# Prologue order of a recursive interaction kernel: c1 chunks ahead of D, weight passes re-ordered, first loads on one queue, D's last stores issued by ScalarE

## The chip, the cores and the metric

One core of a Trainium2 chip. The metric is the device time of one execution in microseconds (us), as the median of several runs.

## The reference

Batch 512, 40 features, depth 16, three layers of 100 units. Cut to what matters:

```python
for Wk, bk in zip([W0, W1, W2], [b0, b1, b2]):
    z = jnp.einsum('bid,bjd->bdij', base, curr)
    curr = jnp.einsum('bdij,ijh->bhd', z, Wk) + bk[None, :, None]
    logit.append(curr)
pooled = jnp.sum(jnp.concatenate(logit, axis=1), axis=-1)
out = pooled @ lin_w + lin_b
```

The kernel uses that only a weighted sum of the third layer is wanted. It forms the products x_a * x_b of all pairs of features (with a feature of ones added, 41 in all) once, and multiplies them by two sets of weights: W0, which gives the first layer (c1), and a set Q folded from W1, W2 and the linear weights, which gives a second factor. The output is the sum over units and depth of c1 times that second factor, plus a constant.

## The kernel before

**Tiles.** The columns are depth times batch; one unit u of the loop is 1024 columns (two depths), 8 units in all. The 861 pairs are laid out as 7 chunks of 126 partitions, so there are 56 chunks, m = 7u + c. For each chunk VectorE multiplies the two x tiles (`form`, L263), ScalarE rounds the product to fp32r (`round_high`, L367), VectorE subtracts to get the rest (`split`, L270), and TensorE multiplies by W0 into c1_ps (`c1_chunk`) and by Q into q_ps (`q_chunk`). Each of these two is three passes of two matmuls (`chunk_products`, L499): high weights by high product, low weights by high product, high weights by low product. Per unit, ScalarE copies c1 out and VectorE multiplies and adds (`product`). The order on each engine is written out by hand; the engines meet by semaphores.

**The first unit.** In the first 30 us everything is built at once. The first tile of x comes in halves: xa by SyncE (L185), xb by ScalarE (`load_first_xb`, L391). For chunks 1 to 5 the x_b rows aren't loaded but selected by TensorE from chunk 0's (`select_xb`, L543) into PSUM, where `form` reads them; chunk 6 is loaded. The weights W0 come as pairs (i, j) and (j, i) in four pieces (`load_w0`, cut at chunks 0, 1, 3, 5): GpSimd adds them (`sum_w0`, L459), ScalarE rounds (`cast_w0`, L386), GpSimd subtracts (`low_w0`, L465).

**Q's weights.** TensorE makes V from W2 and the linear weights (`v_piece`, L558 and L564), ScalarE copies it, TensorE turns it (`turn_v`, L573), ScalarE copies again (L412). Then D = V times W1 in five groups (`d_group`, L588 and L591) in the order 4, 0, 1, 2, 3, using two PSUM banks in turn, so that a group waits for the copy of the one before last. The copies (`copy_d`) are ScalarE's, but for group 2, VectorE's (L301). D goes to DRAM in ten stores (`store_d`, L172): eight issued by SyncE, two by GpSimd behind `dgroup_copied` 3, that is behind the copy of group 1. After all ten have landed and GpSimd has cleared part of the tile (L480, behind its last `low_w0`), twelve gathers bring D back as pairs (`gather_d`, L166): seven issued by SyncE, five by ScalarE, which has them ahead of chunk 7's rounding. VectorE makes the Q weights of chunks 0 to 3 in two pieces (`first_weights`: sum L308, high L311, low L313), GpSimd those of chunks 4 to 6. Behind the gathers SyncE loads the second unit's x. ScalarE raises `q_psum_free`, for which the first Q chunk waits, ahead of chunk 7.

TensorE's own order is: warm-up matmuls, selections 1 and 2, V pieces 0 and 1, c1 chunk 0, V pieces 2 and 3, the constant, selection 3, turning V, selection 4, D groups 4, 0, 1, selection 5, D groups 2, 3, c1 chunks 1 to 6, Q chunks 0 to 6, and from chunk 7 on c1 and Q in turn.

## Time and profile before

| | us |
|---|---|
| median of 3 runs (180.68 to 181.23) | 181.17 |
| profiled execution | 181.1 |
| its span | 179.3 |
| TensorE matmul busy (97%) | 173.2 |
| VectorE busy (86%) | 153.5 |
| ScalarE busy (41%) | 73.1 |
| GpSimd busy (7%) | 13.2 |

The span is the time from the first to the last instruction of the program in one profiled execution; that execution took 1.8 us more than its span. Matmuls are pipelined and their ends are modelled, so what counts for TensorE is where it starts to wait. An entry in square brackets behind an instruction is the idle time of its engine in front of it and what ended it. [...]

### The profile page before, as it was taken

How to read it: one execution, taken by the hardware profiler on the slowest of the kernel's cores; microseconds unless marked ns; L12 is line 12 of the kernel's file. 1: busy time of each engine (PE TensorE's matmuls, PEld its weight loads, DVE VectorE, ACT ScalarE, POOL GpSimd, SP SyncE). 2: the span in 40 equal slices, each digit the busy share in tenths (PEclk: the TensorE clock that was granted, in tenths of full speed). 3: DMA queues.
4: the chain of work that ended last, by engine and by line, in shares of the span. 5: the costliest groups of instructions: out<-in, count | busy, mean ns of one | idle time of the engine just before them, and what ended most of it. 6: DMA issues, size and time to landing. Idle time of an engine off the chain costs nothing.

```text
span 179.3 us, 2565 instructions
## 1 busy us (share of the span) xinstructions
PE 173.2 (97%) x800; PEld 118.2 (66%) x800; DVE 153.5 (86%) x141; ACT 73.1 (41%) x80; POOL 13.2 (7%) x22
## 2 busy tenths in 40 slices
PE   6899987999999999999999999999999999999995
PEld 1273655777777777777777777777777777777762
DVE  0799976399999999999999999999999999994012
ACT  2556710064642464336432644264425542530020
POOL 3253904000000000000000000000000000000000
PEclk9999999999999999999999999999999999999999
DMA  5999744999878677857785779577947740000000
GB/s 165 396 411 399 263 103 121 419 413 412 280 237 301 158 230 230 325 133 236 229 302 163 228 228 310 162 224 236 327 134 227 229 149 0 0 0 4 0 0 0
DMA packets 12636, 37.59 MB, mean 210 GB/s; under 512 B 2548, under 2 KB 3668, under 8 KB 12628
## 3 DMA queue, kind: packets, MB, share of 16 engines
q1 hardware_dynamic: 11408, 36.39, 61.2%
q10 hardware_dynamic: 1156, 0.85, 1.8%
q0 software_dynamic: 64, 0.25, 0.4%
q8 instruction: 5, 0.08, 0.2%
q14 instruction: 3, 0.02, 0.0%
HBM read 36.40 MB, written 1.07 MB: 209 GB/s over the span
## 4 chain that ended last, share of the span: by engine, by line
PE 85%; DMA 6%; DVE 4%; SPq 2%; issue 1%; ACT 0%; DVEq 0%
PE q_ps L499 42%; PE c_ps L499 39%; DMA x_a<-xa 3%; DVE xb_z L263 2%; DMA pair_sb<-d_dram 2%; SPq L172 1%; DMA d_dram<-w_d 1%; PE q_ps L564 1%; PE q_ps L508 1%; PE c_ps L543 1%; SPq L166 1%; PE c_ps L638 1%; PE q_ps L543 1%; PE c_ps L642 0%; DVE acc L356 0%
## 5 line engine op out<-in xcount | busy, mean ns | idle before, releaser
L367 ACT ACTIVATE z_high<-xb_z 126x1024 fp32r<-126x1024 f32 x56 | 59.3, 1061 | 80.2 <-DVE xb_z L263 78.9
L270 DVE TENSOR_TENSOR z_low<-xb_z,z_high 126x1024 fp32r<-126x1024 f32 x56 | 69.2, 1241 | 0.5 <-ACT z_high L367 0.5
L263 DVE TENSOR_TENSOR xb_z<-x_a,xb_z 126x1024 f32<-126x1024 f32 x50 | 61.3, 1226 | 3.3 <-DMA xb_z<-xw 3.2
L499 PE MATMUL c_ps<-z_high,wc_high 126*101 126x512 f32 x112 | 35.3, 396 | 0.6 <-DVE z_low L270 0.6
L499 PE MATMUL c_ps<-z_low,wc_high 126*101 126x512 f32 x112 | 35.0, 394 | 0.0
L499 PE MATMUL c_ps<-z_high,wc_low 126*101 126x512 f32 x112 | 35.0, 393 | 0.0
L499 PE MATMUL q_ps<-z_high,wq_high 126*101 126x512 f32 x108 | 34.0, 396 | 0.9 <-DVE wq_low L313 0.9
L499 PE MATMUL q_ps<-z_high,wq_low 126*101 126x512 f32 x108 | 33.8, 394 | 0.0
L499 PE MATMUL q_ps<-z_low,wq_high 126*101 126x512 f32 x108 | 33.7, 393 | 0.0
L499 PEld LDWEIGHTS c_ps<-z_high,wc_high 126*101 126x101 f32 x112 | 18.3, 165 | 9.0 <-ACT z_high L367 1.1
L499 PEld LDWEIGHTS c_ps<-z_high,wc_low 126*101 126x101 f32 x112 | 18.5, 165 | 7.5
L499 PEld LDWEIGHTS c_ps<-z_low,wc_high 126*101 126x101 f32 x112 | 18.5, 165 | 7.4
L499 PEld LDWEIGHTS q_ps<-z_high,wq_high 126*101 126x101 f32 x108 | 17.8, 165 | 8.5 <-DVE wq_low L313 1.4
L499 PEld LDWEIGHTS q_ps<-z_high,wq_low 126*101 126x101 f32 x108 | 17.9, 165 | 7.3
L499 PEld LDWEIGHTS q_ps<-z_low,wq_high 126*101 126x101 f32 x108 | 17.8, 165 | 7.2
L374 ACT ACTIVATE w_post<-c_ps 101x1024 f32<-101x1024 f32 x8 | 8.1, 1010 | 13.5 <-PE c_ps L499 13.5
L284 DVE TENSOR_TENSOR w_post<-q_ps,w_post 101x256 f32<-101x256 f32 (+1 forms) x3 | 1.4, 508 | 10.5 <-PE q_ps L508 10.5
L280 DVE TENSOR_TENSOR acc<-acc,w_post 101x1024 f32<-101x1024 f32 x7 | 8.6, 1225 | 0.2
L278 DVE TENSOR_TENSOR w_post<-q_ps,w_post 101x1024 f32<-101x1024 f32 x7 | 8.5, 1217 | 0.0
L552 PE MATMUL q_ps<-warm_sb 128*128 128x512 bf16 x14 | 5.7, 587 | 1.6 <-POOL warm_sb L452 1.6
L291 DVE TENSOR_TENSOR xb_z<-x_a,xb_z 126x512 f32<-126x512 f32 x2 | 1.4, 692 | 5.1 <-DMA x_a<-xa 5.1
L552 PEld LDWEIGHTS q_ps<-warm_sb 128*128 128x128 bf16 x14 | 1.5, 104 | 5.4 <-issue 5.4
(59 smaller groups left out, 62.9 us busy)
## 6 DMA issues: line engine op xcount, KB each, us to landing
xb_z<-xw SPq DMA_DIRECT2D x50, 512.0 KB, 4.4
x_a<-xa SPq DMA_DIRECT2D x7, 512.0 KB, 4.8
w_post<-w1x SPq DMA_DIRECT2D x4, 512.0 KB, 8.7
w_d<-w2h SPq DMA_DIRECT2D x4, 404.0 KB, 6.4
pair_sb<-w_pairs SPq DMA_DIRECT2D x3, 202.0 KB, 9.9
xb_z<-xw ACTq DMA_DIRECT2D x2, 256.0 KB, 4.3
x_a<-xa SPq DMA_DIRECT2D x2, 256.0 KB, 4.5
d_dram<-w_d SPq DMA_DIRECT2D x2, 189.4 KB, 3.4
```

Of the source, the lines that this page charges most:

```text
L166: eng.dma_start(q_sides[P * t:P * (t + 1), side, c0 * J:c1 * J].rearrange("p (c j) -> p c j", j=J), src).then_inc(dpair_loaded[piece], 16)
L172: eng.dma_start(d_dram[r0:r1, column * J:(column + n) * J], w2_d[DR * upper + r0:DR * upper + r1, first * J:(first + n) * J]).then_inc(sto ...
L263: nc.vector.tensor_tensor(xb_z[0:K, c, :], x_a[0:K, u % 2, :], x_b, ALU.mult).then_inc(z_done, 1)
L270: nc.vector.tensor_tensor(z_low[0:K, m % SLOTS, :], xb_z[0:K, c, :], z_high[0:K, m % SLOTS, :].bitcast(fp32), ALU.subtract).then_inc(low_d ...
L278: nc.vector.tensor_tensor(prod, q_ps[u % 2][0:J, :], c1_sb[u % 2], ALU.mult).then_inc(q_psum_free, 1)
L280: nc.vector.tensor_tensor(acc[:, :], acc[:, :], prod, ALU.add).then_inc(acc_done, 1)
L367: nc.scalar.activation(z_high[0:K, m % SLOTS, :], xb_z[0:K, m % C, :], ACT.Copy).then_inc(high_done, 1)
L374: nc.scalar.activation(c1_sb[u % 2], c1_ps[u % 2][0:J, :], ACT.Copy).then_inc(c1_copied, 1)
L499: last = nc.tensor.matmul(ps[0:J, h * B:(h + 1) * B], w[0:K, c * J:(c + 1) * J], z[0:K, slot, h * B:(h + 1) * B], start=(c == 0 and k == 0 ...
L508: last = nc.tensor.matmul(q_ps[1][0:J, cols], w[0:K, c * J:(c + 1) * J], z[0:K, slot, cols], start=False, stop=(c == C - 1 and k == 2))
L543: last = nc.tensor.matmul(sel_ps[m % 2][:, cols], select_r[:, m:m + 128], x_split[0:K, cols], start=True, stop=True)
L552: nc.tensor.matmul(warm_ps, warm_sb[:, 0:128], warm_sb[:, :], start=True, stop=True)
```

## The change

- The first halves of xb are issued by SyncE between those of xa, not by ScalarE.
- The second piece of W0 is loaded ahead of W2.
- TensorE: c1 chunk 0 goes ahead of V's pieces and c1 chunk 1 ahead of D's groups; selections 3, 4 and 5 change places (3 ahead of V piece 3, 4 ahead of turning V, 5 behind D's groups); the constant goes behind the first copy of D by VectorE, ahead of c1 chunk 4.
- A chunk's passes are now high by high, high by low product, low weights by high product. The wait for the low products stands ahead of the second pass, the one for low weights ahead of the third; ahead of the first only the high ones are waited for.
- VectorE: forms and splits of the first unit in another order, with the copy of group 2 behind split 3.
- ScalarE: the cast of the second piece of W0 ahead of rounding 2; rounding 3 ahead of the copies of D; rounding 4 between the copies of groups 1 and 3; the constant's copy behind the gathers' issue, with a wait.
- The two stores of group 3 are issued by ScalarE behind its copy of that group, ahead of two casts of W0 and roundings 5 and 6, no longer by SyncE.

```diff
--- before.py
+++ after.py
@@ -184,6 +184,10 @@
                 cols = slice(h * B, (h + 1) * B)
                 sp.dma_start(x_a[:, 0, cols], xa[:, cols]).then_inc(loaded, 16)
 
+            def load_first_xb(h, loaded):
+                cols = slice(h * B, (h + 1) * B)
+                sp.dma_start(xb_z[:, 0, cols], xw[0:128, cols]).then_inc(loaded, 16)
+
             def load_xb(u, c):
                 sp.dma_start(xb_z[:, c, :], xw[c:c + 128, bass.ds(u * N, N)]).then_inc(xb_loaded[c], 16)
 
@@ -200,12 +204,14 @@
                 sp.dma_start(w1_post[:, cols], w1x[:, cols]).then_inc(w1_loaded[i], 16)
 
             load_first_xa(0, xa_first)
+            load_first_xb(0, xb_first)
             load_first_xa(1, xa_loaded[0])
+            load_first_xb(1, xb_loaded[0])
             sp.dma_start(small_sb[:, :], small).then_inc(small_loaded, 16)
             load_w0(0)
+            load_w0(1)
             for i in range(VP):
                 load_w2(i)
-            load_w0(1)
             for i in W1_ORDER:
                 load_w1(i)
             load_w0(2)
@@ -221,9 +227,6 @@
             store_d(sp, 0, LEFT + 2 * GI, 2 * GI, GI, (0, DB))
             store_d(sp, 1, LEFT + UPPER_AT[2], 2 * GI, GI, (DR - DB, DR))
             store_d(sp, 1, 0, 3 * GI - (LEFT - 2 * GI), LEFT - 2 * GI, (0, 32))
-            sp.wait_ge(dgroup_copied, 4)
-            store_d(sp, 0, LEFT + 3 * GI, 3 * GI, GI, (4, 4 + DB))
-            store_d(sp, 1, LEFT + UPPER_AT[3], 3 * GI, GI, (10, 10 + DB))
             sp.wait_ge(equals_cleared, 1)
             sp.wait_ge(d_stored, 16 * DS_SP)
             sp.wait_ge(d_stored_pool, 16 * DS_POOL)
@@ -330,15 +333,16 @@
             form(0, 1)
             form(0, 2)
             split(0, 1)
+            form(0, 3)
             split(0, 2)
-            form(0, 3)
             form(0, 4)
+            split(0, 3)
+            copy_d(2)
+            split(0, 4)
             form(0, 5)
-            copy_d(2)
-            split(0, 3)
             form(0, 6)
-            for m in range(4, C):
-                split(0, m)
+            split(0, 5)
+            split(0, 6)
             first_weights(0)
             first_weights(1)
             products(0, C, 2 * C)
@@ -386,17 +390,11 @@
                 nc.scalar.activation(chunks(wc_high, WC_CUTS[i], WC_CUTS[i + 1]),
                                      w0_sides[0:K, WC_CUTS[i]:WC_CUTS[i + 1], 0, :], ACT.Copy).then_inc(wc_highs, 1)
 
-            def load_first_xb(h, loaded):
-                cols = slice(h * B, (h + 1) * B)
-                act.dma_start(xb_z[:, 0, cols], xw[0:128, cols]).then_inc(loaded, 16)
-
             def round_xa(h, loaded):
                 cols = slice(h * B, (h + 1) * B)
                 act.wait_ge(loaded, 16)
                 nc.scalar.activation(x_split[0:K, cols], x_a[0:K, 0, cols], ACT.Copy).then_inc(xa_high, 1)
 
-            load_first_xb(0, xb_first)
-            load_first_xb(1, xb_loaded[0])
             round_xa(0, xa_first)
             round_xa(1, xa_loaded[0])
             act.wait_ge(small_loaded, 16)
@@ -404,23 +402,26 @@
             round_high(0, 0)
             cast_w0(0)
             round_high(0, 1)
+            cast_w0(1)
             round_high(0, 2)
             act.wait_ge(v_multiplied, 1)
             nc.scalar.activation(v_rows[:, :], v_ps, ACT.Copy).then_inc(v_rows_copied, 1)
-            act.wait_ge(const_done, 1)
             act.wait_ge(v_turned, 1)
             nc.scalar.activation(v_sb[:, :], vt_ps, ACT.Copy).then_inc(v_copied, 1)
-            nc.scalar.activation(const_sb[:, :], const_ps, ACT.Identity, bias=linb,
-                                 scale=float(D)).then_inc(const_copied, 1)
-            cast_w0(1)
+            round_high(0, 3)
             copy_d(4)
             copy_d(0)
             copy_d(1)
-            round_high(0, 3)
+            round_high(0, 4)
             copy_d(3)
+            act.wait_ge(dgroup_copied, 4)
+            store_d(act, 0, LEFT + 3 * GI, 3 * GI, GI, (4, 4 + DB))
+            store_d(act, 1, LEFT + UPPER_AT[3], 3 * GI, GI, (10, 10 + DB))
             cast_w0(2)
             cast_w0(3)
-            for m in range(4, BODY):
+            round_high(0, 5)
+            round_high(0, 6)
+            for m in range(C, BODY):
                 if m == GATHER_AT:
                     act.wait_ge(equals_cleared, 1)
                     act.wait_ge(d_stored, 16 * DS_SP)
@@ -429,6 +430,10 @@
                         if (side, t, piece) not in GATHER_SP:
                             gather_d(act, side, t, piece)
                 if m == C:
+                    act.wait_ge(const_done, 1)
+                    nc.scalar.activation(const_sb[:, :], const_ps, ACT.Identity, bias=linb,
+                                         scale=float(D)).then_inc(const_copied, 1)
+                    act.wait_ge(const_copied, 1)
                     act.wait_ge(z_done, C)
                     act.sem_inc(q_psum_free, 2)
                     act.sem_inc(c1_psum_free, 2)
@@ -491,20 +496,19 @@
 
         @block.tensor
         def _(pe):
-            def chunk_products(ps, high, low, m):
+            def chunk_pass(ps, w, z, m, first, last):
 
                 c, slot = m % C, m % SLOTS
-                for k, (w, z) in enumerate(((high, z_high), (low, z_high), (high, z_low))):
-                    for h in range(2):
-                        last = nc.tensor.matmul(ps[0:J, h * B:(h + 1) * B], w[0:K, c * J:(c + 1) * J],
-                                                z[0:K, slot, h * B:(h + 1) * B],
-                                                start=(c == 0 and k == 0), stop=(c == C - 1 and k == 2))
-                return last
+                for h in range(2):
+                    end = nc.tensor.matmul(ps[0:J, h * B:(h + 1) * B], w[0:K, c * J:(c + 1) * J],
+                                           z[0:K, slot, h * B:(h + 1) * B],
+                                           start=(c == 0 and first), stop=(c == C - 1 and last))
+                return end
 
             def last_q(m, cols):
 
                 c, slot = m % C, m % SLOTS
-                for k, (w, z) in enumerate(((wq_high, z_high), (wq_low, z_high), (wq_high, z_low))):
+                for k, (w, z) in enumerate(((wq_high, z_high), (wq_high, z_low), (wq_low, z_high))):
                     last = nc.tensor.matmul(q_ps[1][0:J, cols], w[0:K, c * J:(c + 1) * J], z[0:K, slot, cols],
                                             start=False, stop=(c == C - 1 and k == 2))
                 return last
@@ -512,24 +516,34 @@
             def c1_chunk(it, m):
                 u, c = divmod(m, C)
                 if m in WC_CUTS[:-1]:
-                    pe.wait_ge(wc_ready, WC_CUTS.index(m) + 1)
+                    pe.wait_ge(wc_highs, WC_CUTS.index(m) + 1)
                 pe.wait_ge(high_done, it * BODY + (m + 1))
-                pe.wait_ge(low_done, it * BODY + (m + 1))
                 if c == 0 and u >= 1:
                     pe.wait_ge(c1_psum_free, it * 2 + (u + 1))
-                last = chunk_products(c1_ps[u % 2], wc_high, wc_low, m)
+                chunk_pass(c1_ps[u % 2], wc_high, z_high, m, True, False)
+                pe.wait_ge(low_done, it * BODY + (m + 1))
+                chunk_pass(c1_ps[u % 2], wc_high, z_low, m, False, False)
+                if m in WC_CUTS[:-1]:
+                    pe.wait_ge(wc_ready, WC_CUTS.index(m) + 1)
+                last = chunk_pass(c1_ps[u % 2], wc_low, z_high, m, False, True)
                 if c == C - 1:
                     last.then_inc(c1_done, 1)
 
             def q_chunk(it, m):
                 u, c = divmod(m, C)
+                if m in PREP_CUTS[:2]:
+                    pe.wait_ge(wq_highs, PREP_CUTS.index(m) + 1)
+                if m == PREP_CUTS[2]:
+                    pe.wait_ge(last_highs, 1)
+                if c == 0:
+                    pe.wait_ge(q_psum_free, it * 2 + (u + 1))
+                chunk_pass(q_ps[u % 2], wq_high, z_high, m, True, False)
+                chunk_pass(q_ps[u % 2], wq_high, z_low, m, False, False)
                 if m in PREP_CUTS[:2]:
                     pe.wait_ge(wq_ready, PREP_CUTS.index(m) + 1)
                 if m == PREP_CUTS[2]:
                     pe.wait_ge(last_ready, 1)
-                if c == 0:
-                    pe.wait_ge(q_psum_free, it * 2 + (u + 1))
-                chunk_products(q_ps[u % 2], wq_high, wq_low, m).then_inc(z_slots_free, 1)
+                chunk_pass(q_ps[u % 2], wq_low, z_high, m, False, True).then_inc(z_slots_free, 1)
 
             def select_xb(m):
 
@@ -578,8 +592,6 @@
                 d_bank = d_ps[place % 2]
                 if place == 0:
                     pe.wait_ge(v_copied, 1)
-                if place == 1:
-                    pe.wait_ge(const_copied, 1)
                 pe.wait_ge(w1_loaded[g], 16)
                 if place > 1:
                     pe.wait_ge(dgroup_copied, place - 1)
@@ -597,22 +609,25 @@
                 warm()
             select_xb(1)
             select_xb(2)
+            c1_chunk(0, 0)
             v_piece(0)
             v_piece(1)
-            c1_chunk(0, 0)
             v_piece(2)
+            select_xb(3)
             v_piece(3)
-            constant()
-            select_xb(3)
+            select_xb(4)
             turn_v()
-            select_xb(4)
+            c1_chunk(0, 1)
             d_group(4)
             d_group(0)
             d_group(1)
-            select_xb(5)
             d_group(2)
             d_group(3)
-            for m in range(1, C):
+            select_xb(5)
+            for m in range(2, C):
+                if m == PREP_CUTS[2]:
+                    pe.wait_ge(dgroup_copied_dve, 1)
+                    constant()
                 c1_chunk(0, m)
             for m in range(C):
                 q_chunk(0, m)
```

## Rows read from the trace of the kernel before

**Rows 1.** The page: its head, clock by slice, and one group by line
```profile
span 179.3 us, 2565 instructions
...
PEclk9999999999999999999999999999999999999999
...
L367 ACT ACTIVATE z_high<-xb_z 126x1024 fp32r<-126x1024 f32 x56 | 59.3, 1061 | 80.2 <-DVE xb_z L263 78.9
```

**Rows 2.** Chain of waits to 45 us: start, duration (us), what
```profile
1.22 5.24 DMA x_a<-xa
...
20.25 0.71 SPq L172
...
21.47 2.09 DMA d_dram<-w_d
...
24.83 2.85 DMA pair_sb<-d_dram
...
28.41 0.38 DVE wq_low L313
...
28.83 10.03 PE q_ps L499 x42
38.86 1.39 PE c_ps L499 x6
```

**Rows 3.** Timeline, TensorE: start, duration, engine, line, work [idle before it <- releaser]
```profile
13.97 0.30 PE L588 MATMUL q_ps<-w_post,v_sb 101*64 101x101 f32 x1
...
17.25 0.13 PEld L588 LDWEIGHTS q_ps<-w_post,v_sb 101*64 101x64 f32 x1 [0.41 <-DMA w_post<-w1x]
...
17.54 0.59 PE L588 MATMUL q_ps<-w_post,v_sb 101*64 101x505 f32 x1
...
28.83 0.71 PE L499 MATMUL q_ps<-z_high,wq_high 126*101 126x512 f32 x2 [0.94 <-DVE wq_low L313]
```

**Rows 4.** Timeline, VectorE, splits (L270) and forms (L263)
```profile
14.46 1.21 DVE L263 TENSOR_TENSOR xb_z<-x_a,c_ps 126x1024 f32<-126x1024 f32 x1
...
18.55 1.74 DVE L270 TENSOR_TENSOR z_low<-xb_z,z_high 126x1024 fp32r<-126x1024 f32 x1
20.21 1.60 DVE L263 TENSOR_TENSOR xb_z<-x_a,xb_z 126x1024 f32<-126x1024 f32 x1
...
36.70 1.22 DVE L270 TENSOR_TENSOR z_low<-xb_z,z_high 126x1024 fp32r<-126x1024 f32 x1
```

**Rows 5.** Timeline, ScalarE and (ACTq) its DMA issues
```profile
0.75 0.90 ACTq L391 DMA_DIRECT2D xb_z<-xw  x2
...
16.10 0.59 ACT L381 ACTIVATE w_d<-q_ps 128x505 f32<-128x505 f32 x1 [0.25 <-PE q_ps L591]
...
18.60 0.59 ACT L381 ACTIVATE w_d<-q_ps 128x505 f32<-128x505 f32 x1 [0.96 <-PE q_ps L591]
19.09 0.62 ACT L386 ACTIVATE wc_high<-pair_sb 126x202 fp32r<-126x202 f32 x2
...
23.62 2.32 ACTq L166 DMA_DIRECT2D pair_sb<-d_dram  x5
```

**Rows 6.** Timeline, GpSimd (L172 stores, L465 low parts, L480 clearing)
```profile
14.31 0.67 POOL L465 TENSOR_TENSOR wc_low<-pair_sb,wc_high 126x202 fp32r<-126x202 f32 x1 [0.85 <-ACT wc_high L386]
17.00 1.14 POOL L172 DMA_DIRECT2D d_dram<-w_d  x2 [2.02 <-ACT w_d L381]
...
17.64 0.50 POOL L172 DMA_DIRECT2D d_dram<-w_d  x1
...
19.54 1.20 POOL L465 TENSOR_TENSOR wc_low<-pair_sb,wc_high 126x202 fp32r<-126x202 f32 x1 [0.34 <-ACT wc_high L386]
...
20.69 1.57 POOL L465 TENSOR_TENSOR wc_low<-pair_sb,wc_high 126x202 fp32r<-126x202 f32 x1
...
22.32 0.17 POOL L480 MEMSET pair_sb<- 42x101 f32 x1
```

**Rows 7.** DMA issues by line: size, us from issue to landing
```profile
d_dram<-w_d POOLq DMA_DIRECT2D x1, 126.2 KB, 4.6
```

## The prediction, made from the kernel before alone

> **What bounds the kernel now.** I read the head of the page first, then the chain of waits, then each engine's timeline up to 30 us. The span is 179.3 us at a granted clock of 9 tenths or more throughout [rows 1]. The chain of waits shows two parts. From 28.83 us on TensorE never waits: 10.03 us of Q matmuls, then chunks of 1.39 us [rows 2], without a gap until the last product. Nothing after 28.83 us changes in amount, so the whole change is worth what it does to one number: **the start of the first Q matmul**. In front of it, read backwards: the weights' split on VectorE (low part 28.41 to 28.79), the gather of D from DRAM (ScalarE's share issued from 23.62 [rows 5], the piece that lands last 2.85 us after 24.83 [rows 2]), the last store of D (issued 21.47, landed 2.09 us later, at 23.56 [rows 2]), D's groups, and the loads of x. TensorE itself is idle for 0.94 us just in front of it [rows 3], with c1 chunks 0 to 6 done. So work moved around on TensorE matters only where D's chain waits for it.
>
> **The change, part by part.**
>
> *Pass order.* A Q chunk now begins with the two passes on the high weights and needs the low weights only 0.93 us later. The high weights are there when the low ones begin, at 28.41; the first matmul started at 28.83 [rows 2]. That removes 28.83 - 28.41 = **0.42 us**, and it is the surest term: no engine is in the way, the low part is done 0.38 us later and is wanted after 0.93. The number of matmuls is the same. A c1 chunk gets one wait ahead of it and one inside it instead of two ahead; the c1 chunks of before carry two waits and Q chunks none, and both take 1.39 us [rows 2], so I take the waits in the loop at nothing. Their bounds: 0, and some 0.04 us (a loop of 14 chunk pairs shows no more than that at its turn) for each of four rounds.
>
> *x's halves on one queue.* SyncE issues xa, xb, xa, xb instead of xa, xa beside ScalarE's xb, xb. One issue is 0.45 us (the two of ScalarE took 0.90 [rows 5]), so small data and the first weights are issued 0.9 us later. The half of xa issued in front of them took 5.24 us to land in a full queue [rows 2], so the issue hides. The last half of xa landed 5.24 us after 1.22, at 6.46; it closes the same four halves in either order, and VectorE wants all four before the second split. I take 0 us; the bounds are -0.5 (halves are no longer interleaved) and +0.5 us (the fourth is issued 0.9 us later). The Trainium skill ("DMA: Bandwidth & Descriptors", "Issuing engines are not separate DMA queues") says that transfers of all issuing engines run on the same 16 DMA engines and only issue time is saved by using several; by that the term is 0 too, and the rule would count against expecting anything from this edit or from the two stores' new queue except their issue time.
>
> *c1 chunks ahead of D.* Chunk 0 trades places with V's first two pieces, which changes no sum. ScalarE gets a cast of 0.31 us (half of 0.62 [rows 5]) ahead of its copy of V's rows, of which some 0.16 is seen, since the copy had waited for rounding 2. D's first group stood behind ScalarE's copy of V and began at 13.97 [rows 3]; TensorE is done turning V some 0.4 us before that. Now c1 chunk 1, 1.39 us, stands **in front of D's first group**: it begins then at 13.97 - 0.56 + 0.16 + 1.39 = 14.96 (0.56: the copy of V and its handing over, under which the chunk runs): D's groups 4, 0 and 1 are 1.0 us later and the copy of group 1 moves from 16.10 to 17.1, its end from 16.69 to 17.7 [rows 5]. But the last two groups were held up by something else: group 3's weights waited for the load of its data until 17.25 and it began at 17.54 [rows 3]. Now it waits for the copy that ends at 17.7 and begins at 17.8. So group 3's copy moves only from 18.60 [rows 5] to 18.85, and group 2's copy on VectorE stays near 18.0. The selection for chunk 5, which went ahead of group 2, comes behind group 3 and ends at 19.4; form 5 is 3 us later than it was.
>
> *The stores.* Before, SyncE issued seven stores behind the copy of group 1, the last at 21.47. Now its last is the third of group 2, issued at 20.25 as before [rows 2]; the two of group 3 leave ScalarE from 19.5 to 20.4 (0.45 each). Before, SyncE's last store took 2.09 us to land [rows 2]; with that and up to 0.4 more, all eight are down at 22.5 to 22.9 instead of 23.56: **0.7 to 1.0 us earlier**. What is late next? Two things, both behind the copy of group 1, which is 1.0 us later. First, GpSimd's stores (issued 17.00 to 18.14 [rows 6]) move to 18.03 and on; the second, begun at 17.64 [rows 6], took 4.6 us to land [rows 7], 17.64 + 1.03 + 4.6 = **23.3**. Second, GpSimd's low parts of W0 and the clearing of the diagonal, which ended at 22.49 [rows 6], and which gathers wait for as well.
>
> *GpSimd against VectorE.* The low part of two chunks took 0.67 us at 14.31 with VectorE from 14.46 on a form that reads PSUM, and 1.20 and 1.57 us at 19.54 and 20.69 [rows 6] while VectorE ran a split and a form that read two SBUF operands; those took 1.74 and 1.60 us instead of 1.22, the PSUM form 1.21 [rows 4]. I read this as turns: each engine's instruction runs alone, some 0.5 us of GpSimd then some 1.15 us of VectorE. Put forward: ScalarE is free of its stores at 20.4, casts chunks 3 and 4 by 20.85 and 5 and 6 by 21.35. The sums are done by 20.95. Form 5 reads PSUM (20.0 to 21.2), so the first low part runs at once, 20.95 to 21.45; form 6 goes next, to 22.6; the second low part to 23.1; the clearing, 0.17 us [rows 6], to **23.3**. Queued behind the two stores on ScalarE are these casts, and roundings 5 and 6; rounding 6 ends at 23.7 (22.65 + 1.06 [rows 1]), so ScalarE's five gathers are issued 0.1 us later than at 23.62. They took 2.32 us for five [rows 5], and SyncE's chain ended last before, so this is covered for 0.6 us or so.
>
> *Sum.* Gather at 23.35 instead of 23.62, less 0.02 for a late start on ScalarE: 0.25 us. Pass order: 0.42. Together **0.67 us**. TensorE is ready for it: its chunk 6 ends at 26.6. c1 7 needs its low part 0.46 us after its start, which was there at 37.92 before [rows 4]; the low part is wanted at 28.16 + 10.03 + 0.46 = 38.65: no stall. The moved constant costs TensorE 0.2 us inside an idle stretch. The profiled execution took 181.1 us for its span of 179.3; 181.1 - 0.67 = 180.43, and the median of the runs is 0.07 above the profiled one: **180.5 us**. A measurement can tell about 0.3%, 0.54 us, from no change.
>
> **The rivals.**
>
> *The gate does not move* (180.75). GpSimd's second store took 4.6 us to land [rows 7] where SyncE's last took 2.09 [rows 2]. If the second lands at 23.6, only the 0.42 of the pass order is left, 181.17 - 0.42. For it: VectorE is more often on two SBUF operands after 18.7 us than it was at 17 to 18. Against: the delay of 1.03 is all that the trace supports.
>
> *GpSimd misses its turn* (slower, 182.0). If the first low part is not under way when form 6 starts at 21.2, it waits for form 6 (22.4), runs to 22.9, then VectorE's split 5 takes its turn to 24.05, the second low part runs to 24.55, and the clearing ends at 24.8. The gather starts 1.2 us later than before: -0.42 + 1.22 = 0.8 us slower. It decides at one point: the cast for chunks 3 and 4 must end before form 6 starts, 20.85 against 21.2, a margin of 0.35 us. Each store issue on ScalarE that takes 0.6 instead of 0.45 eats 0.15 of it, and so does a late first load, which now runs 1 : 1 through V and D. Against it: VectorE may itself wait for a rounding just then and leave the turn to GpSimd. The Trainium skill ("SBUF — State Buffer", "SBUF: two separate sides") states that VectorE with two SBUF operands and GpSimd take a shared port pair by an exclusive lock, the loser waiting for the whole instruction; by that rule a miss costs what is worked out here, and if they shared it by halves instead it would cost 0.3 us or so. The stretched rows agree with the lock.
>
> *The stores were everything* (179.9). If GpSimd's stores need not shift with their issue, and its low part runs while VectorE waits, the gather starts at 22.9 less 0.1: 0.42 + 0.8 = 1.2 us off.
>
> *The clock falls.* TensorE would stand idle from 26.6 to 28.2 us, longer than the gaps of before [rows 3], under which the clock stayed [rows 1]. If it fell, matmuls at 1.2 GHz would add perhaps 1 to 2 us. Nothing in the rows speaks for it.
>
> **How the numbers follow.** Forecast 0.42; the gate does not move 0.25; missed turn 0.17; stores were everything 0.10; late first loads or the clock 0.06. The forecast's own range, 180.2 to 180.7, lies for the larger part beyond 0.54 us; the first rival doesn't reach it. Faster: 0.10 + 0.32 of the 0.42 = 0.42. Same: 0.25 + 0.10 = 0.35. Slower: 0.17 + 0.06 = 0.23. The range takes in the missed turn and all but the end of the fast rival: 179.8 to 182.0.
>
> **What would show it.** In the trace after: the first Q matmul on the high weights starts within 0.05 us of the end of the high cast, whatever else happens. The copy of D's group 1 ends at about 17.7 and group 3's at 19.4. SyncE has six stores, ScalarE two from 19.5. GpSimd's clearing ends at 23.3 and its second low part follows form 6; a clearing at 24.8 is the missed turn. SyncE's first gather at 23.35 us confirms the gate, at 23.6 the first rival. TensorE's chunks keep 1.39 us. The prediction is wrong if the first select matmuls do not start near 8.0 us, or if any gap opens after the first Q matmul.

## The result and the profile after

The changed kernel takes **181.86 us** (median of 10 runs, 181.27 to 183.87) beside 180.64 us for the kernel before, re-measured in the same rounds; the ratio is 1.0087, with a 95% interval of 1.0065 to 1.0109. It is 1.2 us slower. The ratio is higher than the medians make it (1.0068), since it also counts by their length three runs in which TensorE's mean granted clock was 0.990 or 0.991 and which lasted 183.22 to 183.87 us; without them the medians differ by 1.15 us and the means by 1.0. The forecast was 180.5 with a range of 179.8 to 182.0: the time lies inside the range, but on the other side of no change, and the chance given to that was 0.23. The profiled execution took 181.72 us for a span of 179.9.

The chain of waits of the kernel after, to 45 us (start, duration, what):

```profile
17.72 0.60 ACT w_d L385
...
18.61 1.15 POOL d_dram L172 x2
...
19.77 1.89 POOL pair_sb L464 x2
...
21.68 0.38 ACT wc_high L390
...
22.13 2.88 POOL wc_low L470 x2
...
25.06 0.18 POOL pair_sb L485
...
25.26 0.36 SPq L166
...
26.47 2.48 DMA pair_sb<-d_dram
...
29.38 0.28 DVE wq_high L314
...
29.70 9.91 PE q_ps L503 x42
```

The first Q matmul starts at 29.70 instead of 28.83 [rows 2]. Read backwards: it follows the high cast by 0.05 us, as forecast. In front of that stand the gather, issued at 25.26 instead of 23.62, GpSimd's clearing (25.06), its two low parts (22.13 to 25.01), ScalarE's cast (21.68), GpSimd's two sums (19.77 to 21.66), its stores (18.61), and the copy of D's group 1 (17.72). Before, the last store of D stood where the clearing stands now. In this execution it is the chain of the rival of the missed turn, which gave 182.0 us and a clearing ended at 24.8; it ended at 25.23. Three more traces with the same order (e14, e9, e15) show another chain; they stand with e4 and e6 below.

The same stretch in the timelines of VectorE, GpSimd and ScalarE of the kernel after:

```profile
19.32 1.45 DVE L273 TENSOR_TENSOR z_low<-xb_z,z_high 126x1024 fp32r<-126x1024 f32 x1
...
21.82 1.21 DVE L266 TENSOR_TENSOR xb_z<-x_a,xb_z 126x1024 f32<-126x1024 f32 x1
...
19.77 1.88 POOL L464 TENSOR_TENSOR pair_sb<-pair_sb 126x202 f32<-126x202 f32 x2
22.13 2.87 POOL L470 TENSOR_TENSOR wc_low<-pair_sb,wc_high 126x202 fp32r<-126x202 f32 x2 [0.47 <-ACT wc_high L390]
...
23.43 1.56 POOL L470 TENSOR_TENSOR wc_low<-pair_sb,wc_high 126x202 fp32r<-126x202 f32 x1
...
19.56 0.59 ACT L385 ACTIVATE w_d<-q_ps 128x505 f32<-128x505 f32 x1 [0.31 <-PE q_ps L603]
20.18 1.45 ACTq L172 DMA_DIRECT2D d_dram<-w_d  x2
21.68 0.63 ACT L390 ACTIVATE wc_high<-pair_sb 126x202 fp32r<-126x202 f32 x2 [1.53 <-POOL pair_sb L464]
```

The cast began at 21.68, right when ScalarE had both stores out (20.18 + 1.45), and the first low part at 22.13. The chain and the bracket put the cast down to the sums, but the first cast wants only the first sum, and that was done at 21.16. Form 6, with two SBUF operands, had begun at 21.82. So the low part took 1.34 us where 0.5 to 0.6 is its own work, and the second, behind a split, 1.56 (the two together 2.87). The sums have the same mark: the first waited for split 4, which ran from 19.32; both took 1.88 us, where the timeline of before has 1.04 for the two.

The front of the profile differs too. Busy time, clock and DMA of two stretches of 1 us (after the stretch: its length, then PE, PEld, DVE, ACT, POOL, granted clock, DMA share, GB/s), first the kernel before, then after:

```profile
5.00:6.00 1.00, 1.00 (x4) 0.29 (x3) 0.93 (x2) 0.17 (x1) 0.00 (x0) 1.00 1.01 376
6.00:7.00 1.00, 1.00 (x5) 0.23 (x3) 0.52 (x1) 0.52 (x1) 0.00 (x0) 1.00 1.05 395
```

```profile
5.00:6.00 1.00, 1.00 (x4) 0.28 (x3) 0.59 (x1) 0.25 (x1) 0.00 (x0) 1.00 0.96 295
6.00:7.00 1.00, 0.97 (x3) 0.20 (x3) 0.44 (x1) 0.38 (x1) 0.00 (x0) 1.00 0.96 309
```

The DMA engines are about as busy (0.96 where it was 1.01 and 1.05) and move 22% less: 376 and 395 GB/s became 295 and 309. This isn't chance of one execution: from 5 to 7 us the eight traces with one queue have 285 to 332 GB/s and the nine with two 383 to 403, and from 7 to 9 us 339 to 373 against 398 to 419; by 9 to 12 us the two groups meet (404 to 412 and 406 to 419).

### The profile page after: what moved, and what is told of

Its sections match the earlier page's. It is cut to its first block, busy times and chain, and to the rows that moved or that the text cites. A ratio compares the mean times of both kernels' runs of the same rounds, so it can differ in the third digit from the quotient of the medians.

```text
span 179.9 us, 2514 instructions
## 1 busy us (share of the span) xinstructions
PE 173.3 (96%) x800; PEld 117.9 (66%) x800; DVE 152.6 (85%) x141; ACT 73.2 (41%) x80; POOL 13.8 (8%) x22
## 3 DMA queue, kind: packets, MB, share of 16 engines
HBM read 36.40 MB, written 1.07 MB: 208 GB/s over the span
## 4 chain that ended last, share of the span: by engine, by line
PE 87%; DMA 4%; POOL 3%; DVE 2%; SPq 1%; issue 1%; ACT 1%; DVEq 0%
PE q_ps L503 42%; PE c_ps L503 40%; DMA xb_z<-xw 2%; POOL wc_low L470 2%; DMA pair_sb<-d_dram 1%; POOL pair_sb L464 1%; PE q_ps L578 1%; PE q_ps L512 1%; PE c_ps L557 1%; POOL d_dram L172 1%; PE q_ps L557 1%; SPq L166 1%; PE q_ps L603 1%; PE c_ps L653 1%; PE q_ps L600 1%
## 5 line engine op out<-in xcount | busy, mean ns | idle before, releaser
L470 POOL TENSOR_TENSOR wc_low<-pair_sb,wc_high 126x202 fp32r<-126x202 f32 (+1 forms) x4 | 5.5, 1379 | 2.8 <-ACT wc_high L390 2.8
```

The source lines that it names most:

```text
L470: nc.gpsimd.tensor_tensor(chunks(wc_low, c0, c1), w0_sides[0:K, c0:c1, 0, :], chunks(wc_high, c0, c1).bitcast(fp32), ALU.subtract).then_in ...
```

## The experiments

Each ran beside the kernel before on the same chip. "Low clock" counts runs with a mean granted clock below 0.995. The ratio comes from the single runs, not from the two medians; low-clock runs are part of it in after, e4, e6, e8, e13 and e14, so compare medians there too. One run of e8 took 346.5 us and one of e7 970.2 us, for no cause that the record shows; the medians hardly feel them.

| kernel | median us | before beside it | ratio, 95% interval | low clock |
|---|---|---|---|---|
| after | 181.86 | 180.64 | 1.0087 [1.0065, 1.0109] | 3 of 10 |
| e1 before + pass order | 179.92 | 180.71 | 0.9958 [0.9939, 0.9977] | 0 of 12 |
| e2 before + one queue | 181.52 | 180.71 | 1.0031 [1.0003, 1.0059] | 3 of 12 |
| e3 after, two queues | 181.39 | 180.71 | 1.0034 [1.0011, 1.0058] | 1 of 12 |
| e5 after, c1 chunk 1 behind D | 181.21 | 180.71 | 1.0032 [1.0011, 1.0052] | 0 of 12 |
| e4 after, stores on SyncE | 181.76 | 180.45 | 1.0070 [1.0047, 1.0092] | 2 of 12 |
| e6 after, cleared early | 182.09 | 180.45 | 1.0069 [1.0045, 1.0094] | 2 of 8 |
| e8 e1 + stores ahead of casts | 180.40 | 180.45 | 0.9993 [0.9966, 1.0020] | 1 of 12 |
| e7 e1 + stores behind casts | 180.03 | 180.45 | 0.9958 [0.9939, 0.9978] | 0 of 12 |
| e9 after, 16 warm-ups | 181.62 | 180.66 | 1.0069 [1.0041, 1.0097] | 0 of 7 |
| e10 e3 and e5 together | 180.66 | 180.66 | 1.0000 [0.9981, 1.0019] | 0 of 12 |
| e11 e10, stores behind casts | 180.49 | 180.66 | 0.9986 [0.9968, 1.0004] | 0 of 12 |
| e12 e1, 15 warm-ups | 180.04 | 180.66 | 0.9966 [0.9949, 0.9984] | 0 of 12 |
| e13 before, 10 warm-ups | 182.21 | 180.53 | 1.0105 [1.0064, 1.0145] | 4 of 6 |
| e14 after once more | 182.08 | 180.53 | 1.0107 [1.0066, 1.0148] | 2 of 7 |
| e15 after, 16 warm-ups again | 181.98 | 180.53 | 1.0070 [1.0047, 1.0093] | 0 of 8 |

The theory after the result: the first Q matmul is late because GpSimd's work behind group 1's copy is late and then loses a turn to VectorE. Rivals: ScalarE's stores hold the casts; one queue for x makes everything late; the pass order itself costs; and, as e14 will show, the landing of the last store is late by itself.

### e1: the pass order alone

```diff
-                for k, (w, z) in enumerate(((high, z_high), (low, z_high), (high, z_low))):
+                chunk_pass(c1_ps[u % 2], wc_high, z_high, m, True, False)
+                pe.wait_ge(low_done, it * BODY + (m + 1))
+                chunk_pass(c1_ps[u % 2], wc_high, z_low, m, False, False)
...
+                last = chunk_pass(c1_ps[u % 2], wc_low, z_high, m, False, True)
```

> The kernel before with the pass order and its waits alone (high weights by high and by low product first, low weights last; waits split). By my working, the first Q matmul starts behind the high cast and not behind the low part: 0.42 us earlier than in the kernel before. The trace of the changed kernel shows besides that the turns of the loop cost nothing any more (c1 and Q chunks 1.44 us at a turn of before, six turns, 0.05 each): 0.27 us more. Expected: -0.4 to -0.7 us against before, first Q matmul within 0.05 us of the end of the high cast. Rival: passes only look cheaper because TensorE meets a later wait, and the time doesn't move.

Measured: 179.92 us, 0.8 us below the kernel before beside it. It is the fastest kernel of the case, before and after included. The chain of waits at one turn of the loop and at the same place of the next turn, first the kernel before, then e1 (with its first seven Q chunks):

```profile
55.50 1.41 PE c_ps L499 x6
56.91 1.44 PE q_ps L499 x6
58.34 1.39 PE c_ps L499 x6
...
76.39 1.44 PE q_ps L499 x6
```

```profile
28.75 9.91 PE q_ps L498 x42
...
55.24 1.40 PE c_ps L498 x6
56.64 1.39 PE q_ps L498 x6
58.03 1.40 PE c_ps L498 x6
...
76.11 1.39 PE q_ps L498 x6
```

Before, the chain has six such rows of 1.44 us, one at each turn, where the others are 1.37 to 1.41; e1 has none. From the first Q matmul to the end of the span before took 150.5 us (179.3 - 28.83), e1 150.2 (179.0 - 28.75), the changed kernel 150.2 (179.9 - 29.70). But the rows of 1.44 aren't where the time went: a whole round of the loop takes 19.48 us before (76.39 - 56.91) and 19.47 in e1 (76.11 - 56.64), since other chunks of e1 take 1.40 where those of before take 1.38. Up to TensorE's last matmul it is 148.46 or 148.47 us in the three traces with the old pass order and 148.20 to 148.22 in the fourteen with the new one: 0.26 us less, 0.12 of it in the first seven Q chunks (10.03 and 9.91 to 9.93) and 0.14 spread over the rest. The saving is firm; which part of the edit, the order or the place of the waits, makes it was not tried. In the profiled execution of e1 the stores landed 0.6 us later than in that of before (24.17), which hides the 0.42 us at the first Q matmul there; the median has it.

### e2: one queue alone, and e3: the changed kernel with two

```diff
-            load_first_xb(0, xb_first)
-            load_first_xb(1, xb_loaded[0])
...
             load_first_xa(0, xa_first)
+            load_first_xb(0, xb_first)
             load_first_xa(1, xa_loaded[0])
+            load_first_xb(1, xb_loaded[0])
```

The two lines taken out are ScalarE's, those put in SyncE's. e3 is the reverse of this on the changed kernel.

> The kernel before with the four halves of x on SyncE's queue alone. In the changed kernel the 14 loads of the first 20 us land 0.6 to 1.2 us later than before, and the trace moved 295 to 309 GB/s between 5 and 7 us where the kernel before moved 376 to 395. Theory A (one queue is the cause): here too the loads behind x land 0.6 us later or more, D's group 3 and the last store shift by as much, and the time is 0.5 to 0.7 us longer. Theory B (the bandwidth was that of another execution or chip, not of the queue): loads land as in the kernel before, the time is the same within 0.2 us.

> The changed kernel with xb's halves issued by ScalarE again, all else as changed. If one queue costs the 0.6 us, the loads land as before and the copy of D's group 1 ends 0.4 to 0.6 us earlier, near 17.8 us. If the missed turn of GpSimd is a matter of that shift, the clearing ends at 23.3 to 23.6 instead of 25.2 us and the time falls by 1.5 us or so; if the missed turn comes from c1 chunk 1 ahead of D and from what stands on GpSimd behind group 1's copy, only 0.4 to 0.6 us come back.

Measured: e2 takes 181.52 us, 0.8 more than the kernel before (without the low-clock runs 181.42 against 180.62, the same 0.8). e3 takes 181.39, 0.4 less than the changed kernel without low-clock runs (181.37 against 181.79). Both traces for 5 to 7 us, e2 first:

```profile
5.00:6.00 1.00, 1.00 (x5) 0.28 (x3) 0.93 (x2) 0.00 (x0) 0.00 (x0) 1.00 1.03 337
6.00:7.00 1.00, 0.97 (x3) 0.20 (x3) 0.00 (x0) 0.63 (x1) 0.00 (x0) 1.00 0.92 291
```

```profile
5.00:6.00 1.00, 1.00 (x4) 0.30 (x3) 0.99 (x2) 0.37 (x1) 0.00 (x0) 1.00 1.04 391
6.00:7.00 1.00, 1.00 (x5) 0.23 (x3) 0.94 (x3) 0.85 (x3) 0.00 (x0) 1.00 1.09 404
```

e2 has the low rate on the kernel before, e3 the full one on the changed kernel. Theory A holds: it is the queue. In e2 the last piece of W1 landed at 18.05 us instead of 17.20 and the last store of D at 24.43 instead of 23.56. What the queue costs is less firm: 0.8 us by e2's medians, 0.6 by its ratio with an interval from 0.1 to 1.1, 0.4 by e3, which ran beside other runs than the changed kernel did, and 0.55 by e10 against e5. e3 also answers the second question. Group 1's copy began at 17.24 instead of 17.72, and the clearing still ended at 24.75, a turn late. The missed turn does not come from the queue.

### e5: c1 chunk 1 behind D, and e10: with two queues

```diff
-            c1_chunk(0, 1)
             d_group(4)
...
             d_group(3)
             select_xb(5)
+            c1_chunk(0, 1)
```

> The changed kernel with c1 chunk 1 moved behind D's groups and selection 5. If c1 chunk 1 ahead of D is what makes GpSimd late (it cost 1.0 us up to group 1's copy), that copy ends at 17.2 to 17.4 instead of 18.3 us, GpSimd's stores, sums and low parts follow, the clearing ends near 23.5, and the time falls by 1.2 to 1.7 us against the changed kernel, below the kernel before. If ScalarE's two stores hold the casts up instead, the casts stay at 21.6 us and the time comes down by 0.3 us at most.

> The changed kernel with xb's halves on ScalarE again and c1 chunk 1 behind D's groups: both causes on D's path undone, the stores and the orders left. Sum of the single steps: two queues gave 0.4 us, c1 chunk 1 behind D 0.6: 180.8 us. The copy of group 1 should end at 17.0 to 17.3 us. What would be left against 179.9 (the pass order alone) is then the stores ahead of the casts, 0.5 to 0.6 us, and W0's second piece ahead of W2. If it is 181.2 or more, something else in the orders costs.

Measured: e5 181.21 us, 0.6 below the changed kernel; e10 180.66, 0.7 below e3 on full clock (181.37). In e5 group 1's copy ended at 17.84 us (17.2 to 17.4 expected), the clearing at 23.88 (near 23.5 expected), and the casts began at 21.73, held by ScalarE's stores as the rival said. But the gather started at 24.99: the last of those stores had landed at 24.92. The 0.6 us gained are half or less of what the first theory expected (1.2 to 1.7) and twice what the rival allowed (0.3 at most); the rest went to this next gate. In e10 the gate is the same, with the clearing ended just before it (24.02); the chain of waits:

```profile
19.34 4.75 DMA d_dram<-w_d
...
24.16 0.36 SPq L166
```

The DMA on the gate was issued by ScalarE at 19.34 and landed 4.75 us later. So a store that is issued early is not down early. Eight other stores were under way when it was issued; when the last store of the kernel before was issued at 21.47 and landed 2.09 us later, four were.

### e4: the stores back on SyncE, and e6: no wait for GpSimd's low parts

e4 moves the two stores and their wait from behind `copy_d(3)` on ScalarE back to the end of SyncE's stores. e6 gives the gathered pairs a tile of their own (and puts the output into the old one, which isn't shown):

```diff
+        gathered = sb("gathered", [128, 2 * C * J])
-        q_sides = pair_sb.ap().rearrange("p (s n) -> p s n", s=2)
+        q_sides = gathered.ap().rearrange("p (s n) -> p s n", s=2)
...
+            nc.gpsimd.memset(q_sides[0:P, 1, 0:J], 0.0).then_inc(equals_cleared, 1)
...
-            pool.wait_ge(wc_ready, len(WC_CUTS) - 1)
-            nc.gpsimd.memset(q_sides[0:P, 1, 0:J], 0.0).then_inc(equals_cleared, 1)
```

> The changed kernel with group 3's two stores issued by SyncE again, behind its others. In the changed kernel ScalarE's second store was in issue until 21.63 us and the cast of the third W0 piece began at 21.68, though its sum had been ready at 21.16. Theory C (the stores on ScalarE hold the casts): the casts start at 21.2, GpSimd's low parts a turn earlier, the clearing ends 0.5 us or more earlier, and SyncE's own last store lands at 25 us or later, so that the stores become the gate; the time within 0.3 us of the changed kernel. Theory D (what is late is all on GpSimd, behind group 1's copy): the clearing stays at 25.2 us; the time doesn't fall.

> The changed kernel with the gathered pairs in a tile of their own, cleared at the start by GpSimd, so that the gather waits for the stores alone and for ScalarE to be free, and no longer for GpSimd's low parts. In the changed kernel the last store landed at 24.58 us and the clearing ended at 25.23. If the low parts' missed turn is the gate, the gather starts at 24.6 instead of 25.26 and the time is 0.6 us shorter than the changed kernel's, but still as long as before's or a little longer, since the stores too land 1.0 us later than before's 23.56. If the stores were the true gate, no change.

Measured: e4 181.76 us, no change from the changed kernel. Its chain of waits and GpSimd's timeline:

```profile
22.55 2.36 DMA d_dram<-w_d
...
21.70 0.58 POOL L470 TENSOR_TENSOR wc_low<-pair_sb,wc_high 126x202 fp32r<-126x202 f32 x1
...
23.86 0.18 POOL L485 MEMSET pair_sb<- 42x101 f32 x1
```

The casts began at 21.25, the first low part at 21.70 and took 0.58 us: it caught its turn, and the clearing ended at 24.04, 1.2 us earlier than in the changed kernel. That is what theory C forecast. It also bears out the exclusive lock of the Trainium skill ("SBUF — State Buffer", "SBUF: two separate sides"): the same instruction took 0.58 us where it came before VectorE's and 1.34 where it came behind. But SyncE's own last store was issued at 22.55 and landed at 24.91, and the gather started at 24.98. Either gate is late by itself; taking one away leaves the other 0.3 us behind it. e6 took 182.09 us, 181.94 without its low-clock runs: no gain, as its rival (the stores are the true gate) said. Its profiled execution is one with a low clock and can't be compared step by step; there the gather waited for a store. That the low parts' turn alone is worth 0.6 us is **not shown**.

Three further traces speak against it. e14 is the changed kernel unaltered; e9 and e15 differ from it by two warm-up matmuls. The chain of waits of e14, and GpSimd's timeline:

```profile
20.00 1.33 SPq L172
21.37 3.23 DMA d_dram<-w_d
...
24.67 0.36 SPq L166
...
21.82 0.58 POOL L470 TENSOR_TENSOR wc_low<-pair_sb,wc_high 126x202 fp32r<-126x202 f32 x1
...
23.98 0.18 POOL L485 MEMSET pair_sb<- 42x101 f32 x1
```

The first low part began at 21.82, ahead of form 6 (22.00), took 0.58 us, and the clearing ended at 24.16, all with the two stores still on ScalarE. So e4's caught turn doesn't need e4's edit. The gather waited until 24.67 for SyncE's third store of group 2, issued at 21.37 and landed 3.23 us later. In e9 and e15 the clearing ended at 23.87 and 24.44, and the gather started at 25.17 and 25.56, behind stores that landed at 25.11 and 25.50. GpSimd missed its turn in one of four traces of this order; in the other three the landing of a store was the gate, and in the first too it was only 0.65 us behind the clearing (24.58). Nor does the time follow the turn: the execution that missed it took 181.72 us, the three that didn't 181.26, 181.62 and 182.15.

### e8 and e7: the stores on ScalarE, on a kernel that is otherwise good

```diff
-            sp.wait_ge(dgroup_copied, 4)
-            store_d(sp, 0, LEFT + 3 * GI, 3 * GI, GI, (4, 4 + DB))
-            store_d(sp, 1, LEFT + UPPER_AT[3], 3 * GI, GI, (10, 10 + DB))
...
             copy_d(3)
+            act.wait_ge(dgroup_copied, 4)
+            store_d(act, 0, LEFT + 3 * GI, 3 * GI, GI, (4, 4 + DB))
+            store_d(act, 1, LEFT + UPPER_AT[3], 3 * GI, GI, (10, 10 + DB))
             cast_w0(2)
             cast_w0(3)
```

(e7 has the three lines behind the casts.)

> The kernel before with the pass order (179.9 us) and, besides, group 3's two stores issued by ScalarE right behind its copy, ahead of the casts, as in the change. By my working of the stores, all are down at 22.5 to 22.9 us; in this kernel c1 chunk 1 isn't ahead of D and GpSimd isn't late. If the casts aren't held, the gather starts near 23 and the time is 0.5 to 0.8 us below the pass order alone (179.2). If ScalarE's issue holds the casts by 1 us and GpSimd then misses its turn, the clearing ends at 23.7 to 24.5 and nothing or less is gained (179.9 to 180.4).

> As the one before, but with the two stores behind ScalarE's two casts and ahead of rounding 4: the casts can't be held, the stores are issued 0.6 us later (from 19.8 us). Expected by the theory of the held casts: clearing at 22.5 as in the kernel before, stores landed near 23.2 to 23.6, time 0.3 to 0.7 us below the pass order alone. By the rival (landing is set by the DMA queues and not by who issues): stores land near 24, the time is that of the pass order alone, 179.9.

Measured: e8 180.40 us, that is the time of before, so the whole 0.4% of the pass order is gone; e7 180.03, with e1's ratio of 0.9958. The chain of e8, and e7's:

```profile
19.93 0.84 ACTq L172
...
20.81 0.39 ACT wc_high L383
...
21.26 2.90 POOL wc_low L465 x2
...
24.21 0.19 POOL pair_sb L480
...
24.42 0.36 SPq L166
```

```profile
18.65 1.52 SPq L172
...
20.22 3.19 DMA d_dram<-w_d
...
23.48 0.36 SPq L166
```

e8 shows the mechanism with nothing else changed: store 0.84 us in issue, the cast behind it at 20.81 instead of 19.18 in e1, two low parts of 2.90 us together, the clearing, the gather at 24.42. e7 has the casts free, and its gate is SyncE's third store of group 2: it could be issued only at 20.22, behind one that took 1.52 us, and landed 3.19 us later. Its traced gather starts at 23.48, but its median is e1's within 0.1 us. (e1's profiled execution, 180.78 us, lay 0.9 above its median, so the traces of the two don't compare.) The expectation by the theory, 0.3 to 0.7 us below the pass order alone, missed. The stores on ScalarE bring nothing there. Ahead of the casts they cost 0.4 us by the medians of e8 and e7, which ran side by side, and 0.35% by the ratios, whose intervals overlap a little.

### e11: the changed kernel with all three mended

> As the one before, with ScalarE's two stores behind its two casts. If the stores ahead of the casts cost what they cost on the kernel before (0.5 us), 180.3 us, and the clearing ends before the last store has landed; if the gate is the stores' landing by now, no gain, 180.8.

Measured: 180.49 us, 0.9986 [0.9968, 1.0004]. The 0.1% gained on e10 (0.2 us by the medians) is within the intervals. The casts were free (from 19.93 us) and the clearing ended at 22.72, but the gather waited until 23.74 for ScalarE's second store, landed at 23.68. Against e7 (0.9958), which has the stores in the same place, the other moves of the change (selections, forms and splits, W0's second piece, the constant) would cost 0.28%, 0.5 us; the two intervals overlap, and which move it would be was not tried.

### e9, e12 to e15: the clock

All change WARM alone, the number of warm-up matmuls (e12 on e1, e13 on the kernel before, the others on the changed one).

> The changed kernel with 16 warm-up matmuls instead of 14. In the trace of the changed kernel TensorE is idle for 1.01 us between the warm-up and the first selection (0.76 before the change), and 3 of its 10 runs have a mean clock of 0.991 and last 183.2 to 183.9 us instead of 181.8. In one trace of an experiment with such a clock the clock stood at half for 3.4 us from 8.6 us on, after 1.74 us of idle time there. Theory: that idle stretch is what lets the clock fall; with two more matmuls it shrinks to 0.3 us, no run of 12 has the lower mean clock, and the median of the others stays at 181.8. Rival: the clock falls for another cause (the idle before the first Q matmul, or the chip): 2 to 4 of 12 runs still show it.

> A version to beat both kernels: the kernel before with the pass order alone and 15 warm-up matmuls instead of 14. Expected 179.9 us as without the added matmul (it runs where TensorE was idle for 0.5 to 0.8 us), and no run with a lower mean clock. If the 15th matmul delays the first selection, 180.0 to 180.3.

> The kernel before with 10 warm-up matmuls instead of 14: TensorE is idle 1.5 us longer ahead of the first selection (2.3 instead of 0.8 us), nothing else changes. Theory (that idle stretch lets the clock fall): far more runs than before's 4 in 95 have a mean clock of 0.991 or less, each some 2 us longer; if most have, the median goes to 182.5. Rival (another cause): one run of 12 at most, median 180.6.

> The changed kernel once more, unaltered, beside the next one on the same chip. Median 181.8, 2 to 4 of 12 runs with a clock of 0.991 and 183 us or more. If none has it, the share depends on the chip.

> The changed kernel with 16 warm-up matmuls again, for more runs. Theory of the idle stretch: no run with a low clock, median of the rest within 0.2 us of the one before. Rival: as many low runs as the one before.

Measured: the count is in the table. The trace of e6 and that of e13 caught the fall. TensorE's timeline at the first selection, and the granted clock of three stretches, for e6 and then e13:

```profile
8.85 1.19 PE L557 MATMUL c_ps<-z_high,select_r 126*128 126x512 f32 x2 [1.74 <-DVE z_high L300]
...
5.20:8.60 3.40, 1.88 (x6) 0.43 (x5) 2.01 (x4) 1.40 (x3) 0.47 (x1) 1.00 0.95 326
8.60:12.00 3.40, 3.15 (x8) 2.35 (x9) 2.98 (x4) 1.16 (x3) 2.08 (x3) 0.51 1.03 407
12.00:16.00 4.00, 4.00 (x77) 2.74 (x75) 2.87 (x3) 2.04 (x4) 1.35 (x1) 0.99 1.03 412
```

```profile
8.02 0.71 PE L543 MATMUL c_ps<-z_high,select_r 126*128 126x512 f32 x2 [1.98 <-DVE z_high L296]
...
8.60:12.00 3.40, 3.40 (x40) 2.46 (x39) 3.40 (x4) 1.20 (x2) 1.26 (x2) 0.61 1.05 412
12.00:16.00 4.00, 4.00 (x49) 2.58 (x49) 3.58 (x3) 1.95 (x6) 1.67 (x2) 0.90 1.02 409
```

TensorE stood idle for 1.74 and 1.98 us ahead of the first selection, and the granted clock went from 1.0 (2.4 GHz) to 0.5 (1.2 GHz): at 8.6 us in e6, still in the idle stretch, and between 9 and 10 us in e13, when TensorE had been at work again for over 1 us. It was back by 12 or shortly after. e2's trace has an idle stretch of 1.84 us at the same place and no fall, so the stretch alone doesn't decide it. In e6 the pair of selections took 1.19 us instead of 0.70. Such runs of the changed kernel last 183.2 to 183.9 us, 1.4 to 2.1 more than its median without them.

Counted over all runs: kernels with one queue and 14 warm-ups 12 of 61 (after, e14, e2, e4, e5, e6); with 16 warm-ups 0 of 15; the kernel before 5 of 109; with 10 warm-ups 4 of 6; the kernels with two queues, the new pass order and 14 warm-ups (e1, e3, e7, e8, e10, e11) 2 of 72. The two extra warm-ups cut the idle stretch from 1.0 to 1.3 us (after and e14) to 0.2 to 0.8 us (e9 and e15). Fewer warm-ups clearly raise the share. More warm-ups point the same way, but at a share of 12 in 61, none in 15 would come up by chance about once in 27 times. So the idle stretch ahead of the first selection goes with the fall of the clock, and in the kernel before making it longer brought the fall on. In e13 the four low-clock runs took 182.0 to 182.6 us, 1.5 to 2.1 more than the kernel before beside it, but its two others 181.4 and 183.9, of which I have no account. With 16 warm-ups the median hardly moves (181.98 in e15 beside 182.08 in e14); the tail is what goes. e12 took 180.04 us, no better than e1, which had no low-clock run either.

## Why the prediction was wrong

**The step that failed in every trace is the landing of D's last store.** The sum had SyncE's and ScalarE's stores down at 22.5 to 22.9 us, GpSimd's at 23.3, and the gather at 23.35. In the four traces of this order the last store landed at 24.58, 24.60, 25.11 and 25.50 (23.56 before) and the gather started between 24.67 and 25.56. (GpSimd's landed at 23.39, as forecast.) Two queues again, c1 chunk 1 behind D as well, and the stores behind the casts as well brought it to 24.20, 24.10 and 23.68 (e3, e10, e11), so as far as single traces can tell three terms fed it: one queue for x, c1 chunk 1 ahead of D, and the price of a store.

**Pass order: right in mechanism, too small.** 0.42 us by the high cast; e1 shows 0.8 us (ratio 0.9958). The step "I take the waits in the loop at nothing" allowed only for a cost, and for four rounds where the chain shows six turns; measured is a gain of 0.26 us behind the first Q matmul, 0.12 of it in the first seven Q chunks. With 0.42 that makes 0.7. Why those chunks are shorter is open.

**One queue: the first step that failed.** I took 0 with bounds of 0.5 us. e2 shows 0.8 us on the kernel before (0.6 by the ratio), e3 0.4 on the changed one. The working counted bytes ("the same four halves in either order") and asked whether issues hide. They do: nothing waited for an issue. What changed is the rate up to about 9 us; why is open. The rule of the Trainium skill ("DMA: Bandwidth & Descriptors", "Issuing engines are not separate DMA queues") that several issuing engines only save issue time would make this term 0 as well; here the measurement decides against it, with 285 to 332 GB/s on one queue and 383 to 403 on two.

**c1 chunk 1 ahead of D: right in size, wrong in what followed.** It was forecast to put group 1's copy 1.0 us later, ending at 17.7; it ended at 18.31, the rest from the queue (17.83 in e3, with two). Then I said that it matters only up to group 3's load. e3 against e10 shows 0.7 us (e5 against the changed kernel 0.6): what stands behind group 1's copy, GpSimd's stores, sums and low parts, was taken for uncritical, and in e5 the clearing came 1.35 us earlier (23.88).

**The stores: wrong.** "0.45 each" was taken from loads issued at the very start. The two took 1.45 us, and SyncE's third of group 2 waited behind one of 1.57; the last store landed at 24.58, not at 22.9. Landing times of 2.1 to 2.5 us were taken from the last store of before, which went out with four others under way; with seven or eight under way the last one took 2.87 us in the changed kernel, 3.19 in e7 and 4.75 in e10. In e8, where D isn't late, all were down at 23.50, still not at 22.9.

**GpSimd's turn: the rival's time was met, its mechanism in one trace of four.** The forecast had the cast done at 20.85, 0.35 us ahead of form 6. I named what would eat the margin and then took each by itself. The copy was 0.6 us late, the sums lost a turn behind split 4 and were done at 21.66 where the forecast had 20.95, and the stores held ScalarE to 21.63. The clearing ended at 25.23. In e14, e9 and e15 the stores left ScalarE in time and the turn was caught, yet those executions took 181.26 to 182.15 us, because the last store landed later than the clearing ended. So the rival's 182.0 lies near the measured 181.86 in part by luck: a second gate stood where it had put the first. The turn does hang on a margin of a few tenths, as the rival said: the low part came 0.31 us behind form 6 in the one trace and 0.18 ahead of it in e14.

**The clock** was placed in front of the first Q matmul, where the idle stretch is 0.96 us and nothing happens. It falls around the first selection. The last half of x, for which that waits, landed at 7.19 us in e6 and 7.30 in e2, but at 6.47 in the profiled execution of the changed kernel, as before (6.46); I had no term for that stretch.

The sum with the measured terms, in us against the kernel before: pass order -0.7 to -0.8 (e1), one queue +0.4 to +0.8 (e3, e2), c1 chunk 1 +0.6 to +0.7 (e5, e3 against e10), stores ahead of the casts +0.2 to +0.4 (e10 against e11, e8 against e7), the rest 0 to +0.5 (e11 against e7). That gives 0.4 to 1.7, and 1.2 was measured. Most of these terms are about as large as their intervals, and with several gates close together they need not add, so the sum agrees but proves no single term.

## What to carry to other kernels

A time set by one waiting point has several chains behind it; before moving work, list the second and third latest and what would make each late, since here two gates stood within 0.7 us and removing one (e4, e6) gained nothing. A DMA issue on a compute engine is not a fixed price: it held the casts behind it for 0.5 us in the profiled execution, 1.3 in e8 (19.52 to 20.81) and next to nothing in e14, so whatever decides the next stage goes ahead of it. Put the wait for a late operand behind the passes that don't need it: that was the one part of this change that paid. And take a second trace of the same kernel before building on a chain: here it had another gate.

## What the runs showed of the hardware that was not expected

- With the four 256 KB halves on one queue, the DMA engines were nearly as busy (0.92 to 1.06 by their rows, against 1.03 to 1.07) but moved 285 to 332 GB/s instead of 383 to 403 from 5 to 7 us, in eight traces against nine, and 339 to 373 instead of 398 to 419 from 7 to 9 us, when it was almost all other loads than x's halves.
- The issue of a store took from 0.32 to 1.57 us on SyncE and 0.36 to 1.05 us on ScalarE in the changed kernel. Its two long ones overlapped and ended within 0.03 us of each other (21.66 and 21.63), and so did those of e3 (20.99 and 20.95) and e14 (21.33 and 21.32). What both waited for is open.
- TensorE's clock fell to 1.2 GHz around the first selection in the two traces that caught it, with idle stretches of 1.74 us (e6) and 1.98 us (e13) just before, but not in e2's with 1.84. With 10 warm-up matmuls instead of 14 on the kernel before, the share of such runs rose from 5 of 109 to 4 of 6.
